# Three attentions over heads of 8: input loaded inside the first stage, first batch through six PSUM banks, decay table early, no wait of the PE for SyncE's sign

## The reference

```python
x = x + L0_attn_a(layernorm(x))   # rms: q and k normalised per head
x = x + L0_ffn(layernorm(x))      # mixture of 8 experts, 2 per token
x = x + L0_attn_b(layernorm(x))   # decay
x = x + L0_ffn(layernorm(x))
x = x + L1_attn_a(layernorm(x))   # relative: bucketed position bias
x = x + L1_ffn(layernorm(x))      # experts choose their tokens
x = x + L1_attn_b(layernorm(x))   # wide: 16 heads of 64
x = x + L1_ffn(layernorm(x))
```

```python
write_lines = exterior(x_prev @ w1_write.T, x @ w2_write.T)  # 6 numbers per token and head
read_lines = exterior(x @ w1_read.T, x @ w2_read.T)
incidence = einsum("bqhp,bkhp->bhqk", read_lines, write_lines @ J6)
weights = sigmoid(decay_logits)[h] ** (q - k)  where q > k, else 0
logits = q @ k.T * scale + incidence * weights * bias_scale[h]
```

## Time and profile before

| | us |
|---|---|
| median of 3 runs | 6526.69 (6521.57 to 6538.94) |
| the profiled execution, its own time | 6507.51 |
| its span, first to last instruction | 6505.7 |
| first transfer of the rms stage issued at | 18.11 |
| first transfer of the decay stage issued at | 1285.51 |
| first transfer of the relative stage issued at | 2835.73 |
| PE busy in the span | 4965.4 (76%) |
| DVE busy | 3701.5 (57%) |
| ACT busy | 3366.0 (52%) |
| POOL busy | 1256.0 (19%) |

### The profile page before, as it was taken

One profiled execution on the slowest core, in us unless ns is written; L12 is line 12 of the kernel. 1 busy time (PEld: TensorE's weight loads), 2 busy tenths in 40 slices (PEclk: granted clock), 3 DMA queues, 4 the chain that ended last, 5 costly groups with the idle time before them and its releaser, 6 DMA issues. The chain is left out here.

```text
span 6505.7 us, 95125 instructions
## 1 busy us (share of the span) xinstructions
PE 4965.4 (76%) x29755; PEld 2574.5 (40%) x30008; DVE 3701.5 (57%) x7740; ACT 3366.0 (52%) x5243; POOL 1256.0 (19%) x1147
## 2 busy tenths in 40 slices
PE   5999718748888842948777846689999999999466
PEld 1333318724444432932222234433333334343444
DVE  4333344467767763556666666167666666756561
ACT  4888515425555531627666702266666666666122
POOL 1000033333334305321111006500000000000056
PEclk9999858869999966979999957799999999999577
DMA  3333511213333341132222122300000000000214
GB/s 79 73 76 79 81 37 51 69 40 89 88 85 90 90 60 43 50 82 60 59 63 65 49 61 41 71 1 0 0 0 0 0 0 0 0 0 0 61 33 91
DMA packets 297981, 311.38 MB, mean 48 GB/s; under 512 B 60950, under 2 KB 248566, under 8 KB 297604
## 3 DMA queue, kind: packets, MB, share of 16 engines
q1 hardware_dynamic: 265180, 269.54, 17.0%
q0 software_dynamic: 32448, 37.39, 2.9%
HBM read 193.60 MB, written 112.80 MB: 47 GB/s over the span
## 5 line engine op out<-in xcount | busy, mean ns | idle before, releaser
L953 ACT ACTIVATE prob_relative<-slot_relative 128x1024 f32<-128x1024 f32 x512 | 500.0, 1042 | 146.9 <-PE obank_relative L827 140.5
L3300 ACT ACTIVATE prob_wide<-slot_wide 128x1024 f32<-128x1024 f32 x512 | 493.8, 1016 | 149.7 <-PE slot_wide L3199 149.7
L1271 DVE TENSOR_TENSOR slot_decay<-slot_decay,dtab_decay 128x512 f32<-128x512 f32 (+3 forms) x1024 | 453.9, 493 | 168.1 <-PE slot_decay L787 148.4
L953 ACT ACTIVATE prob_rms<-slot_rms 128x1024 f32<-128x1024 f32 x512 | 498.0, 1040 | 85.3 <-PE slot_rms L802 83.4
L953 ACT ACTIVATE prob_decay<-slot_decay 128x640 f32<-128x640 f32 x512 | 358.6, 705 | 344.7 <-PE slot_decay L808 344.0
L3199 PE MATMUL slot_wide<-qT_wide,kT_wide 64*128 64x512 f32 x2048 | 508.8, 615 | 2.9 <-ACT prob_wide L3300 2.9
L2675 POOL DMA_INDIRECT xg_choice_b<-xn_rows_choice_b,ids_choice_b x64 | 85.4, 1334 | 2072.6 <-DVE ids_choice_b L2951 2053.4
L1283 DVE TENSOR_TENSOR prob_relative<-prob_relative,rtab_relative 128x512 f32<-128x512 f32 (+1 forms) x512 | 409.8, 849 | 128.3 <-ACT prob_relative L953 119.0
L3212 PE MATMUL obank_wide<-prob_wide,v_wide 128*64 128x512 f32 x2048 | 467.7, 598 | 1.8 <-DVE zT_wide L3357 1.8
L827 PE MATMUL obank_relative<-prob_relative,vaug_relative 128*32 128x512 f32 x2048 | 291.7, 644 | 116.6 <-DVE prob_relative L1283 115.0
L3343 DVE TENSOR_TENSOR sums_wide<-sums_wide,prob_wide 128x1024 f32<-128x1024 f32 x256 | 313.6, 1225 | 28.7 <-ACT prob_wide L3300 0.2
(11 more groups left out here) (748 smaller groups left out, 10320.7 us busy)
## 6 DMA issues: line engine op xcount, KB each, us to landing
scratch_decay<-parts_decay SPq DMA_DIRECT2D x192, 128.0 KB, 2.4
qst_rms<-scratch_rms SPq DMA_DIRECT2D x64, 288.0 KB
kst_rms<-scratch_rms SPq DMA_DIRECT2D x192, 96.0 KB
qst_relative<-scratch_relative SPq DMA_DIRECT2D x64, 288.0 KB
kst_relative<-scratch_relative SPq DMA_DIRECT2D x192, 96.0 KB
qst_decay<-scratch_decay SPq DMA_DIRECT2D x128, 128.0 KB
scratch_rms<-parts_rms SPq DMA_DIRECT2D x96, 128.0 KB, 2.3
kst_decay<-scratch_decay SPq DMA_DIRECT2D x192, 64.0 KB
```

The lines of the kernel that those rows point to most:

```text
L953: nc.scalar.activation(prob[:, Q % 2, j, 0:c1 - c0], slot[:, u % 3, c0:c1], ACT.Exp).then_inc(exp_done, 1)
L1271: last = nc.vector.tensor_tensor(sl, sl, dtab[:, h, 0:m], ALU.mult)
L3300: nc.scalar.activation(prob[:, Q % 2, u % 4, :], slot[:, u % 2, :], ACT.Exp).then_inc(exp_done, 1)
```

## The change

- The block that loads `X` is gone. The rms stage issues batch 0 of the input first, then its own weights, then batch 1 and the other 14 batches. STATS waits for the batch that it reads.
- In `first_part`, QKV, LINE and TURN_QK no longer share `bench`; they go to the six banks of `slot` (`step_bank`, `line_bank`), and the PE doesn't wait for `bench` there.
- STATS 1 of rms and relative takes batch 1 alone. The other 14 batches come in seven pieces of 8 tiles inside batch 0's attention (SUMS, at units 3, 7, ... 27), and their roots at unit 31 (ROOTS). In the decay stage STATS 1 remains whole.
- SIZE, PEAK and BOUND stand ahead of STATS 1. In the decay stage both LINE steps stand ahead of QKV, and ROOT behind the first two TURN_QK.
- The decay table is made earlier: ACT's 16 exponentials before the first TURN_X, DVE's 16 products in two halves, behind STATS 0 and at EXT.
- `kst` of rms and relative is filled with ones in one fp32 memset of POOL. In the decay stage ACT fills `kin` and `kst`.
- PE waits for three signs; SP gives one in the relative stage only.
- A function `feed_forward` that nothing called is removed.

```diff
+    def spare_bank(i):
+        return slot[:, i % 3, i // 3 * S:(i // 3 + 1) * S]
+    def step_bank(b, i):
+        return spare_bank(i) if at_start(b, -1) else bench[:]
+    def line_bank(b, half):
+        return spare_bank(4 + half) if at_start(b, -1) else bench[:]
-    READY = 4
+    READY = 4 if relative else 3
...
+    if nxt and not prev and not decay:
+        for i in range(1, NB // 2):
+            put(4 * i - 1, "SUMS", i)
+        put(4 * (NB // 2) - 1, "ROOTS")
...
 @block.sync
+    if rms:
+        sp.dma_start(X[:, 0:TPB], x_in[:, 0:TPB]).then_inc(x_first, 16)
     for dst, src in loads:
         sp.dma_start(dst, src).then_inc(loaded, 16)
+    if rms:
+        sp.dma_start(X[:, TPB:2 * TPB], x_in[:, TPB:2 * TPB]).then_inc(x_second, 16)
+        for b in range(2, NB):
+            at = slice(b * TPB, (b + 1) * TPB)
+            sp.dma_start(X[:, at], x_in[:, at]).then_inc(x_rest, 16)
...
 if step == "QKV":
-    bench_free()
-    nc.tensor.matmul(bench[:, 0:3 * D], ...)
+    if not at_start(b, -1):
+        bench_free()
+    nc.tensor.matmul(step_bank(b, t)[:, 0:3 * D], ...)
...
 # POOL
-    link(nc.gpsimd.memset(kst[:].bitcast(F32), 0.0))
-    link(nc.gpsimd.memset(kst[KR // 32 * 32:KS], 1.0))
-    if decay:
-        link(nc.gpsimd.memset(kin[:].bitcast(F32), 0.0))
+    if not decay:
+        nc.gpsimd.memset(kst[:].bitcast(F32), BF16_ONES).then_inc(keys_set, 1)
...
 # ACT, ahead of the walk
+    if decay:
+        fill = [(kin[:], 0.0), (kst[0:KR], 0.0), (kst[KR:P], BF16_ONES)]
+        for rows_, value in fill:
+            v = rows_.rearrange("p h s -> p (h s)").bitcast(F32)
+            last = nc.scalar.activation(v, xnT[0:v.shape[0], 0:1].to_broadcast(list(v.shape)), ACT.Copy, bias=value)
...
+        act.wait_ge(setup_dve, 3)
+        for h in range(H):
+            nc.scalar.activation(dtab[:, h, :], ahead, ACT.Exp, scale=lnd[:, 0, h:h + 1]).then_inc(tab_act, 1)
...
 # DVE
+    def decay_table(heads):
+        for h in heads:
+            dve.wait_ge(tab_act, 3 + h)
+            last = nc.vector.scalar_tensor_tensor(out=dtab[:, h, :], in0=dtab[:, h, :],
+                scalar=bs_t[:, h:h + 1], in1=past, op0=ALU.mult, op1=ALU.mult)
+        link(last)
...
+        if decay and a[0] == 0:
+            decay_table(range(H // 2))
+    if step == "EXT" and at_start(b, -1):
+        decay_table(range(H // 2, H))
```

790 lines of the change are left out of this document (74 added, 716 removed).

## The result

The changed kernel takes 6489.34 us (median of 6 runs, 6485.74 to 6500.05) against 6538.89 us for the kernel before, run beside it (6521.57 to 6562.06): ratio 0.9923, 95% interval 0.9906 to 0.9939. That is 49.6 us faster. I had forecast 72 us, and a time of 6455, so the kernel is 34 us slower than my number.

What follows compares the result with a forecast made beforehand. No engine was busy all the time; three serial stage prologues were taken as the cost. Rms 35, decay 18 and relative 18 make 71, plus 1 for the clock: 72 off 6526.7 gives 6454.7, stated as 6455, range 6434 to 6474.

Steps and rivals of the forecast that it cites:

- The saving is a fixed number of us, so the median goes to 6526.7 - 72: Whole kernel: the median lies 19.2 us above the profiled execution, and the 72 us saved come off it, giving 6454.7.
- the 1 us for the clock: QKV and LINE: the PE reaches its higher clock level when they run without gaps, saving 1 us.
- Decay: 18 us: Decay stage: earlier fills, EXT and table bring DVE's sign 17.3 us earlier; 18 us saved, bounds 13 and 25.
- Rms: Rms stage: first scores 41.4 us earlier, less 6.2 given back in batch 0; 35 us saved.
- The give-back in batch 0: Rms, first batch: moved statistics pieces and roots lengthen it by 6.2 us, 3.0 of it the roots before NRM.
- The statistics' 16 us: Rms prologue: the tile part of the statistics, 16 us, shrinks to a fifteenth ahead of the first scores.
- Relative: Relative stage: memset 6.8, QKV 2.0 and statistics 16.0 us won, 7 given back; 18 us saved.
- The higher clock in the projections: QKV and LINE: running without gaps, they let the PE reach its higher clock level, 1 us saved.
- The sign: Rms prologue: SP's sign after its last STACK issue would cost 4.8 us and is no longer waited for.
- An input that isn't hidden: Rival, rms start: weights queue among 4 MB of input; 10 us more, 6465, chance 0.07.
- Statistics paid in full: Rival, rms and relative: moved statistics cost 19 us in each stage; 25 us more, 6480, chance 0.1.
- The slow side: Rival: a stall of batch 0 drops the PE to 1.2 GHz for later batches; 6567 with three, chance 0.02.

Runs made afterwards that it cites:

- sets 2 to 4: Three later groups of follow-up runs, each on one chip with the unchanged kernel before beside them: 6509.52, 6507.87 and 6507.86 us for that kernel.
- set 3: Later group of follow-up runs on one chip; the kernel before took 6507.87 us there, the unchanged changed kernel 6450.47 us.
- changed again: The changed kernel, unchanged, profiled in a later set of runs: span 6447.6 us, measured 6450.47 us, ratio 0.9916 to the kernel before.
- shift_19: Changed kernel plus 19 PE instructions that wait for nothing, at the end of decay's prologue: 6439.57 us, ratio 0.9890 to the kernel before.
- set 2: Later group of follow-up runs on one chip; the kernel before took 6509.52 us there (7 runs).

## Why the prediction was right and wrong

- **"The saving is a fixed number of us, so the median goes to 6526.7 - 72" failed**, and this step by itself takes the number out of the range. I took all stages that the change doesn't touch to stay as long as in the profile of before, and the median to lie 19.2 above the profiled execution. The profile of before had both choice stages short, so the 19.2 were none of my terms: in sets 2 to 4 the kernel before takes 6507.86 to 6509.52, like its profile. Profile against profile, the pair of the result shows 20.2 us and not 72: unchanged stages take back 35 (choice_b 27.8, choice_a 3.9, wide 2.6, the first mixture 0.7), and decay, rms and relative fall 12.2, 2.4 and 1.3 short, with the 1 us for the clock. The median of the changed kernel lies only 2.0 above its profiled execution, which hides 17.2 of these 52 us and leaves the 34.6 by which it is over 6454.7. The kernel before was slower too in the runs of the result, 6538.89 for 6526.69, so 12.2 of the 34.6 aren't a matter of the saving. In set 3, without the long stages, the times show 57.4, and the profile of before against changed again 58.1, with 0.5 in unchanged stages. The 6450.47 us there would have been near my 6455: that is luck, as 19.2 us of constant that weren't there stand against the 14.6 that the saving lacks.
- **"Decay: 18 us" failed**, in what the step left out. The prologue gave more than forecast: fills 10.8 us (12.3 forecast), the first turned tokens 6.7 earlier (4.9), EXT's end 9.1 earlier (4.6) although the table slowed it, GUARD's start 22.9 earlier (17.3). The gain at EXT comes mostly from LINE and QKV, 7.8 us to the last drain in place of 11.5. The step ended there and took the loop as fixed. The shorter code ahead of the loop moved its jump, and 16 to 18 us were given back: 1018.6 and 1016.7 us, against 1000.7 with 19 instructions put back.
- **Rms: right.** 32.6 and 34.1 for 35. First scores 44.15 for 44.4, of which 0.5 had no row behind it (my sum stood at 43.9). The PE's first product came at 8.76 for 7.7, which the memset until 12.0 hid. The give-back in batch 0 was 8.5 for 6.2: the wait for NRM is 4.8 us and not 3. The statistics' 16 us were mis-attributed: only 12.4 reach the first scores.
- **Relative: right.** 16.7 and 16.8 for 18. First scores 61.3 us behind the start, 58 forecast: ACT's sign was last (1.54 us), not DVE's. Given back 5.0 in batch 0 and 2.5 in the next two, for 7.
- **The higher clock in the projections** (1 us): in rms it didn't come in time. The eight products take 4.92 us (7.3 forecast, with the last drain), one every 0.64, since products in a row don't pay the end of each pair; the views give a granted clock of 1.00 there, but the records of the clock begin only at 22.2 us. In decay it came: the window 1281.75 to 1284.50 has 1.00, the 4.4 us of LINE ahead of it 0.50, and the same eight products take 2.75 us.
- **The sign** (4.8 us): 4.9 at the first scores.
- **The rivals.** An input that isn't hidden costs 11 us (10 forecast) and didn't happen. Statistics paid in full didn't happen, though only four gaps of DVE in batch 0 were clearly longer than a piece (2.5 to 5.6 us), where I had counted six. The slow side, a clock that stays low, I had placed in batch 0; it happened in the last stage, for 28 us, and that the change brought it isn't shown. Its 6567 was also added up wrongly: three times 40 us on 6455 are 6575.
- With the code's place restored, the change gives 69.9 us (shift_19 against before, set 2), for the 72 forecast. That is luck in part: decay's prologue gave 5.6 us more than its term, which covers what rms and relative lack.

## What to carry to other kernels

A loop whose body is too long to be kept is loaded anew in each turn and can wait at its jumps, even over code that never runs; look in the transfers for instruction packets inside a loop, and count such a loop's length and the place of its jumps before a change is priced as an edit of a prologue. Compare stage by stage with two profiles of each kernel before a constant is laid between profile and median. DVE work put "into gaps" of a batch cost there more than half of what it took off the prologue (8.5 of 12.4 us in rms, 7.5 of 13.2 in relative).

## What I had not expected of the hardware

- The PE loads a loop anew above a limit between 1566 and 1722 instructions (1366, 1403 and 1566: no packets in the loop; 1722, 2266 and 2271: packets in every turn). A jump back then costs 2.7 to 3.2 us, with the jump over GUARD behind it mostly 5.8 to 7.5 in decay.
- 19 instructions ahead of a loop moved its stage by 16 to 18 us; 450 instructions for each batch that never run moved theirs by 96.
- The same products took 255.7 or 286.3 us of the PE by the granted clock, in two executions of the same code; the low stretches follow waits of 0.2 to 1.2 us.
- Three fills of 4096 columns took 3.6 us each on ACT.
